# Eight-headed attention: a tile's rows are turned and its logits formed two units on instead of three, in batches of 4, 4, 3, 2, 1, 1, 1 tiles

## The chip, the cores and the metric

The kernel runs on one core of a Trainium2 chip. The metric is the device time of one execution in microseconds, the median of several runs. A core has TensorE (PE, matmuls), VectorE (DVE), ScalarE (ACT), GpSimd (POOL) and SyncE (SP, which here only issues DMAs). Each works through its own queue in order; they meet by semaphores.

## The reference

The whole is a small network on x, 8 x 256 rows of 512 numbers: `x + cross-attention`, `x + gated FFN in fp8`, `x + eight-headed attention`, `x + mixture of experts`. The change lies in the third step and in the routing of the fourth:

```python
def _L1_xattn_ref(q, k, v, gamma):          # eight heads of 32
    qk = jnp.einsum('bhdq,bhdl->bhql', qh, kh) * scale
    sm = jax.nn.softmax(qk, axis=-1)
    ret = jnp.einsum('bhql,bhdl->bhdq', sm, vh)
    return gamma * ret.reshape(B, Dv, Lq)

def _L1_ffn_ref(x, gate_w, gate_b, bias, w1, b1, w2, b2):   # 8 experts, the best 2 of each row
    scores = xf @ gate_w.T + gate_b + bias
    top_scores, top_idx = jax.lax.top_k(scores, TOP_K)
    gates = jax.nn.softmax(top_scores, axis=-1)
    ...
x = x + _L1_xattn_ref(_layernorm(x, axis=-1), ctx_2048, ctx_2048, L1_xattn_gamma)
x = x + _L1_ffn_ref(_layernorm(x, axis=-1), ...)
```

## The kernel before, in words

The kernel has three stages: cross-attention with the FFN (to about 354 us), `head_attention` (to about 655 us) and `experts`. All that follows is in `head_attention`.

x lies in SBUF as `X`, 16 tiles of 128 rows. A **unit** u is the work that updates tile u: four heads at a time (HU = 4) against four chunks of 128 keys (TC = 4), so 16 **steps** (STEPS), worked off in pairs in 8 **cycles** i. A step is one matmul of `scores` into one of two PSUM banks `B[t % 2]`, and an exponential by ScalarE (`weights`) out of it. Every use of B has a number t in the table `turn`, and TensorE may start use t only when ScalarE has finished use t - 2 (semaphore `b_ok`). So `turn` is the order of work on B, and TensorE's and ScalarE's loops must both follow it. Besides the 16 scores, B serves in each unit:

- `mix(u)`, before step 12 (ROWS_AT): the logits of one tile (`logits`, 8 matmuls), the ranks of a batch (`rank`) when one is due, and the turned maxima for the next unit (`rows`);
- `turn_rows(u - 2)`, at the end of unit u: the normalised rows `xn` of tile u - 2 are transposed on TensorE, and ScalarE's `turned_out` copies them to `xt`. The logits of that tile are formed in `mix(u + 1)`, three units after the tile's own.

In the cycles TensorE also does `product` and `row_sums` by turns (the weights times the values, and their sums), and in each odd cycle one `a_quad`: four small matmuls that give the plain scores of a later unit, of which VectorE takes the maxima (`maxima`, two reductions for each quad) before the exponentials need them. In cycles 1 and 3 they are quads 2 and 3 of unit u + 1, in cycles 5 and 7 quads 0 and 1 of unit u + 2. A quad may overwrite its banks only when the maxima of the one before are taken (`max_ok`).

VectorE's order in unit u is: maxima of quad 2; `row_statistics(u - 2)`; maxima of quad 3; `normal_rows(u - 2)`, which writes `xn`; statistics for unit u + 3; maxima of quad 0; `normalise(u - 1)`; maxima of quad 1; queries for unit u + 3; and after that the routing of a batch of tiles, if due: `choose(n)` (the two best experts) in one unit, `gates(n)` and `place_batch(n)` (weights, and the place of each row in its expert's list) in the next. GpSimd adds the result to X (`add`), makes the bf16 parts of queries and keys, gives `1/sqrt` of the variance (`row_power`, between row_statistics and normal_rows), and issues the indirect DMAs that `send` the rows of a batch to `slots_x`, two for each tile. ScalarE's `totals(u - 1)` in cycle 2 empties the bank that `row_sums` of unit u, cycle 3, writes.

The batches before are 4, 4, 3, 3, 1, 1 tiles; the first three are routed inside the loop. The others come behind it, in a tail that ends with `tile_table`, and when the last rows are sent SyncE loads the first tiles of the experts (`load_tile`, a transposing DMA, L1035).

## Time and profile before

| | us |
|---|---|
| median of 3 runs | 848.23 (848.21 to 849.34) |
| profiled execution | 840.42 |
| its span, first to last instruction | 838.7 |
| TensorE busy in the span | 740.9 |
| head_attention, units 2 to 15 | 388.33 to 622.24 |
| its tail, to the first matmul of the experts | 622.24 to 656.95 |

The profile is one execution. A time such as 457.00 is the start of an instruction, counted from the start of the span. An instruction of TensorE that is shown for a group of matmuls has the duration of the group; as matmuls are pipelined, the next group can begin a little before it ends. L1292 and the like are lines of the kernel before.

### The profile page before, as it was taken

How to read it: one execution, taken by the hardware profiler on the slowest of the kernel's cores; microseconds unless marked ns; L12 is line 12 of the kernel's file. 1: busy time of each engine (PE TensorE's matmuls, PEld its weight loads, DVE VectorE, ACT ScalarE, POOL GpSimd, SP SyncE). 2: the span in 40 equal slices, each digit the busy share in tenths (PEclk: the TensorE clock that was granted, in tenths of full speed). 3: DMA queues.
4: the chain of work that ended last, by engine and by line, in shares of the span. 5: the costliest groups of instructions: out<-in, count | busy, mean ns of one | idle time of the engine just before them, and what ended most of it. 6: DMA issues, size and time to landing. Idle time of an engine off the chain costs nothing. (4 is left out here: it accounts for less than half of the span.)

```text
span 838.7 us, 14270 instructions
## 1 busy us (share of the span) xinstructions
PE 740.9 (88%) x4265; PEld 307.1 (37%) x4265; DVE 583.1 (70%) x1096; ACT 399.2 (48%) x744; POOL 358.8 (43%) x356
## 2 busy tenths in 40 slices
PE   3888888799999999798999999989972599999993
PEld 1433433344444444211222222222221355555551
DVE  3577877879594959576888888998947255555552
ACT  1344444365463636256778767866771222222220
POOL 1544455502102031254665668568476033334332
PEclk9899999999999999979999999999995799999998
DMA  7799745002818197134243345444344578999864
GB/s 253 282 131 219 264 174 189 1 0 63 309 59 312 41 344 275 53 92 116 72 112 96 98 128 163 104 116 141 89 160 154 90 106 129 119 134 133 136 88 63
DMA packets 114150, 117.51 MB, mean 140 GB/s; under 512 B 54808, under 2 KB 78232, under 8 KB 113824
## 3 DMA queue, kind: packets, MB, share of 16 engines
q1 hardware_dynamic: 102976, 94.48, 40.4%
q0 software_dynamic: 10384, 22.02, 15.4%
q8 instruction: 36, 0.59, 0.3%
q14 instruction: 34, 0.28, 0.1%
q10 hardware_dynamic: 720, 0.13, 0.1%
HBM read 43.61 MB, written 59.56 MB: 123 GB/s over the span
## 5 line engine op out<-in xcount | busy, mean ns | idle before, releaser
L1397 ACT ACTIVATE t_room<-l_b 128x512 f32<-128x512 f32 x256 | 139.1, 594 | 44.4 <-PE l_b L1292 43.6
L1905 POOL DMA_INDIRECT out<-ex_y,t_tag x39 | 61.7, 1583 | 121.7 <-DMA out<-ex_y,t_tag 70.9
L1801 PE MATMUL ex_hp<-w1h,h_stack 128*128 x312 | 77.2, 317 | 17.2 <-issue 16.7
L1470 DVE TENSOR_REDUCE l_negm<-l_a 128x2 f32<-128x1024 f32 x64 | 75.2, 1219 | 11.1 <-PE l_a L1237 11.1
L1821 PE MATMUL ex_yp<-w2h,ex_ht 128*128 (+1 forms) x234 | 76.2, 380 | 4.9 <-DVE ex_ht L1865 4.7
L1840 ACT ACTIVATE ex_hf<-ex_pre 128x352 f32<-128x352 f32 x39 | 19.4, 496 | 117.1 <-DVE ex_pre L1860 117.1
L1470 DVE TENSOR_REDUCE h_negm<-l_a 128x2 f32<-128x1024 f32 x56 | 65.9, 1220 | 10.5 <-PE l_a L1237 10.3
L1303 PE MATMUL l_pv<-t_room,l_vt 128*32 128x512 f32 x512 | 71.6, 633 | 0.1
L1311 PE MATMUL l_sm<-t_room,ones_f 128*32 128x512 f32 x512 | 69.0, 611 | 0.0
L790 PE MATMUL ps_st<-f_xt,wg 128*128 128x512 fp8e4 x256 | 65.7, 379 | 2.7 <-ACT f_y L838 2.7
L790 PE MATMUL ps_r<-f_xt,wg 128*128 128x512 fp8e4 x256 | 65.7, 379 | 0.0
L936 POOL TENSOR_TENSOR X<-X,f_y 128x512 f32<-128x512 f32 x16 | 19.5, 1221 | 89.9 <-ACT f_y L838 89.9
L1870 DVE TENSOR_TENSOR ex_hl<-ex_hf,ex_hh 128x352 bf16<-128x352 f32 x39 | 20.6, 528 | 43.9 <-ACT ex_hh L1843 42.8
L1801 PE MATMUL ex_hp<-w1l,h_stack 128*128 x156 | 49.4, 317 | 0.0
L823 ACT ACTIVATE f_gate<-ps_st 128x512 bf16<-128x512 f32 x64 | 38.2, 596 | 21.9 <-PE ps_st L790 20.6
L876 DVE TENSOR_TENSOR f_prod<-f_gate,f_up 128x512 bf16<-128x512 bf16 x64 | 26.9, 421 | 29.0 <-ACT f_up L825 26.9
L1292 PE MATMUL l_b<-h_stack 97*128 97x512 bf16 x128 | 42.6, 409 | 3.7 <-DMA h_stack<-h_mrow 2.8
L825 ACT ACTIVATE f_up<-ps_r 128x512 bf16<-128x512 f32 x64 | 38.2, 597 | 15.4 <-PE ps_r L790 15.2
L1821 PE MATMUL ex_yp<-w2l,ex_ht 128*128 (+1 forms) x117 | 44.3, 378 | 0.0
L1878 DVE TENSOR_SCALAR ex_y<-ex_yp,t_tag 128x512 f32<-128x512 f32 x39 | 29.3, 750 | 20.0 <-issue 11.8
L1801 PEld LDWEIGHTS ex_hp<-w1h,h_stack 128*128 128x128 bf16 x312 | 30.9, 99 | 32.0 <-issue 17.5
L1292 PE MATMUL l_b<-l_stack 97*128 97x512 bf16 x128 | 40.3, 385 | 0.8 <-ACT l_xt L1386 0.5
(257 smaller groups left out, 1500.2 us busy)
## 6 DMA issues: line engine op xcount, KB each, us to landing
slots_x<-empty SPq DMA_DIRECT2D x8, 2376.0 KB, 11.0
slots_x<-empty SPq DMA_DIRECT2D x7, 2112.0 KB, 13.0
h_stack<-h_parts SPq DMA_DIRECT2D x96, 64.0 KB
l_stack<-l_parts SPq DMA_DIRECT2D x96, 64.0 KB, 2.0
f_stage<-in_w SPq DMA_DIRECT2D x8, 704.0 KB, 7.2
w1l<-in_ctx SPq DMA_DIRECT2D x8, 512.0 KB, 7.4
f_stage<-in_w SPq DMA_DIRECT2D x8, 512.0 KB
h_kf<-in_ctx SPq DMA_DIRECT2D x16, 256.0 KB, 3.2
```

Source lines behind the costliest of these rows:

```text
L790: mm = pe.matmul(bank[m % 2][:, :], wg8[:, c, col:col + P], xt8[:, c, :], start=c == 0, stop=c == FC - 1)
L823: act.activation(gate[m % 2][:, :], GP[m % 2][:, :], ACT.Gelu_apprx_tanh).then_inc(gate_ok, 1)
L825: act.activation(up[m % 2][:, :], UP[m % 2][:, :], ACT.Copy).then_inc(up_ok, 1)
L1292: pe.matmul(B[t % 2][:, :], stack[u % 2][0:M0 + 1, 0, h, c * P:(c + 1) * P], stack[u % 2][0:M0 + 1, 1, h, :], start=True, stop=True).then_ ...
L1303: mm = pe.matmul(PV[cols, :], VT[u % 2][:, c, cols], weights_at(u, c, h)[:, :], start=c == 0, stop=c == TC - 1)
L1311: mm = pe.matmul(SM[cols, :], ones_f[:, 0:DH], weights_at(u, c, h)[:, :], start=c == 0, stop=c == TC - 1)
L1397: act.activation(weights_at(u, c, h)[:, :], B[t % 2][:, :], ACT.Exp, scale=SCALE).then_inc(b_ok, 1)
L1470: dve.tensor_reduce(negm[u % 2][:, 2 * half:2 * half + 2, j], A[half][:, :, :], AX.X, ALU.max, negate=True)\
L1801: mm = pe.matmul(HP[i % 2][:, 0:H], xt[i % AHEAD][:, xp * FC + f, :], w1p[wp][:, bass.ds(e, 1), f * H:(f + 1) * H], start=k == 0, stop=k = ...
L1821: mm = pe.matmul(YP[i % 2][:, :], ht[i % 2][0:K, n, m, :], w2p[wp][0:K, bass.ds(e, 1), m * D:(m + 1) * D], start=k == 0, stop=k == 3 * HC - 1)
L1878: dve.tensor_scalar(y[i % YS][:, :], YP[i % 2][:, :], tags[i % TAGS][:, bass.ds(e + 1, 1)], None, ALU.mult)\
L1905: pool.indirect_dma_start(out=out, out_offset=bass.IndirectOffsetOnAxis(ap=tags[i % TAGS][:, 0:1].bitcast(U32), axis=0), in_=y[i % YS][:, ...
```

## The change

- The 16 tiles are routed in batches of 4, 4, 3, 2, 1, 1, 1; four of them (INSIDE) within the loop.
- TensorE turns the rows of tile u - 2 before step 6 of unit u (TURN_AT), no longer behind step 15, and ScalarE copies them out there. Their logits are formed in `mix(u)`, not `mix(u + 1)`; `choose`, `gates`, `place_batch`, `gate_weights` and `send` of a batch each come one unit earlier.
- On VectorE `row_statistics(u - 2)` goes ahead of the maxima of quad 2, and `normal_rows(u - 2)` behind them, ahead of the maxima of quad 3.
- On GpSimd `row_power(u - 2)` goes ahead of the sends.
- Behind the loop there is one mix less, and the batches of two, one, one and one are interleaved with the last rows in a new order.

```diff
-    BATCHES = [range(0, 4), range(4, 8), range(8, 11), range(11, 14), range(14, 15), range(15, 16)]
+    BATCHES = [range(0, 4), range(4, 8), range(8, 11), range(11, 13), range(13, 14), range(14, 15), range(15, 16)]
+    INSIDE = 4
+    TURN_AT = 6
 
     turn = {}
     for u in range(NU):
         for s in range(STEPS):
+            if s == TURN_AT and u >= 2:
+                turn["turned", u - 2] = len(turn)
             if s == ROWS_AT:
                 turn["mix", u] = len(turn)
             turn["scores", u, s] = len(turn)
-        if u >= 2:
-            turn["turned", u - 2] = len(turn)
...
     for j in range(NU):
-        turn["logits", j] = turn["mix", j + 3]
-    for n in range(3):
-        turn["ranks", n] = turn["mix", BATCHES[n][-1] + 4]
+        turn["logits", j] = turn["mix", j + 2]
+    for n in range(INSIDE):
+        turn["ranks", n] = turn["mix", BATCHES[n][-1] + 3]
...
@@ tensor @@
+                    if i == TURN_AT // 2 - 1 and u >= 2:
+                        turn_rows(u - 2)
                     if i == ROWS_AT // 2 - 1:
                         mix(u)
-                    if i == CYCLES - 1 and u >= 2:
-                        turn_rows(u - 2)
...
             product(NU - 1, TC - 1)
             row_sums(NU - 1, TC - 1)
+            turn_rows(NU - 2)
+            last_rank(4)
             mix(NU)
-            turn_rows(NU - 2)
-            last_rank(3)
+            turn_rows(NU - 1)
+            last_rank(5)
             mix(NU + 1)
-            turn_rows(NU - 1)
-            last_rank(4)
-            mix(NU + 2)
-            last_rank(5)
+            last_rank(6)
@@ scalar @@
                     weights(u, 2 * i + 1)
+                    if i == TURN_AT // 2 - 1 and u >= 2:
+                        turned_out(u - 2)
...
-                        if i == 7:
-                            turned_out(u - 2)
@@ vector @@
             for u in range(NU):
+                if u >= 2:
+                    row_statistics(u - 2)
                 if u + 1 < NU:
                     maxima(u + 1, 2)
+                if u >= 2:
+                    normal_rows(u - 2)
...
-                if u >= 2:
-                    row_statistics(u - 2)
                 if u + 1 < NU:
                     maxima(u + 1, 3)
-                if u >= 2:
-                    normal_rows(u - 2)
...
-                for n in range(3):
-                    if u == BATCHES[n][-1] + 3:
+                for n in range(INSIDE + 1):
+                    if u == BATCHES[n][-1] + 2:
                         choose(n)
-                    if u == BATCHES[n][-1] + 4:
+                    if n < INSIDE and u == BATCHES[n][-1] + 3:
                         gates(n)
                         place_batch(n)
             row_statistics(NU - 2)
             normal_rows(NU - 2)
-            choose(3)
+            gates(4)
+            place_batch(4)
             normalise(NU - 1)
-            gates(3)
-            place_batch(3)
+            choose(5)
             row_statistics(NU - 1)
             normal_rows(NU - 1)
-            choose(4)
-            gates(4)
-            place_batch(4)
-            choose(5)
             gates(5)
             place_batch(5)
+            choose(6)
+            gates(6)
+            place_batch(6)
             tile_table()
@@ gpsimd @@
                     queries(u + 2)
-                if u == 8:
+                if u >= 2:
+                    row_power(u - 2)
+                if u == 7:
                     pool.wait_ge(cleared, CLEARS)
                 for n in range(3):
-                    first = BATCHES[n][-1] + 5
+                    first = BATCHES[n][-1] + 4
...
-                if u >= 2:
-                    row_power(u - 2)
...
             add(NU - 2)
             row_power(NU - 2)
+            send(3, BATCHES[3])
             with_reciprocals(NU - 1)
-            low_rows(NU - 2)
             add(NU - 1)
             row_power(NU - 1)
-            send(3, BATCHES[3])
+            send(4, BATCHES[4])
+            low_rows(NU - 2)
+            send(5, BATCHES[5])
             low_rows(NU - 1)
-            send(4, BATCHES[4])
-            send(5, BATCHES[5])
+            send(6, BATCHES[6])
```

## Rows read from the trace of the kernel before

**Rows 1.** The page, part 1: busy us (share of the span) and instructions.
```profile
PE 740.9 (88%) x4265; PEld 307.1 (37%) x4265; DVE 583.1 (70%) x1096; ACT 399.2 (48%) x744; POOL 358.8 (43%) x356
```

**Rows 2.** Windows, units 6 to 8: us, busy PE, PEld, DVE, ACT, POOL, PEclk, DMA.
```profile
453.72:469.41 15.69, 15.65 (x115) 4.26 (x111) 12.83 (x17) 12.05 (x25) 9.58 (x12) 1.00 0.42 103
469.41:486.47 17.06, 16.24 (x116) 4.38 (x113) 15.88 (x36) 12.42 (x28) 10.27 (x14) 1.00 0.35 91
486.47:506.11 19.64, 17.63 (x115) 4.41 (x111) 17.39 (x36) 12.12 (x25) 13.49 (x15) 0.91 0.49 138
```

**Rows 3.** Waits of TensorE, 403 to 606 us: total us, times, longest.
```profile
PE l_a L1237 <- DVE l_negm L1470: 3.9, 4, 1.2
```

**Rows 4.** Timeline of TensorE, unit 6, cycles 1 to 3: start, us, instructions.
```profile
457.00 0.39 PE L1237 MATMUL l_a<-l_parts 32*128 32x512 bf16 x4
...
458.86 0.60 PE L1292 MATMUL l_b<-h_stack 97*128 97x512 bf16 x2
459.40 1.06 PE L1311 MATMUL l_sm<-t_room,ones_f 128*32 128x512 f32 x8
```

**Rows 5.** Timeline of VectorE, unit 6, from the maxima of quad 1.
```profile
453.83 2.36 DVE L1470 TENSOR_REDUCE l_negm<-l_a 128x2 f32<-128x1024 f32 x2 [0.96 <-PE l_a L1237]
456.10 0.54 DVE L992 TENSOR_SCALAR h_qf<-X,h_mv,h_rstd 128x512 f32<-128x512 f32 x1
457.43 2.36 DVE L1470 TENSOR_REDUCE l_negm<-l_a 128x2 f32<-128x1024 f32 x2 [0.80 <-PE l_a L1237]
459.70 0.68 DVE L1482 BATCH_NORM_STATS2 l_rst<-X 128x6 f32<-128x512 f32 x1
...
460.83 2.36 DVE L1470 TENSOR_REDUCE l_negm<-l_a 128x2 f32<-128x1024 f32 x2
463.10 0.54 DVE L1493 TENSOR_SCALAR l_xn<-X,l_rmv,l_rrstd 128x512 f32<-128x512 f32 x1
463.55 0.69 DVE L983 BATCH_NORM_STATS2 h_st<-X 128x6 f32<-128x512 f32 x1
```

**Rows 6.** Timeline of GpSimd, unit 6: row_power.
```profile
460.97 0.55 POOL L1663 TENSOR_TENSOR l_rrstd<-l_rveps,neg_half 128x1 f32<-128x1 f32 x1 [2.42 <-DVE l_rveps L1486]
```

**Rows 7.** Timeline of TensorE and ScalarE: totals in unit 6, the turn at its end.
```profile
458.73 0.60 ACT L1408 ACTIVATE l_sums<-l_sm 128x512 f32<-128x512 f32 x1
...
468.49 0.66 PE L1283 MATMUL l_b<-ident_f,l_xn 128*128 128x128 f32 x4
...
469.19 0.60 ACT L1386 ACTIVATE l_xt<-l_b 128x512 f32<-128x512 f32 x1 [0.71 <-PE l_b L1283]
...
469.41 0.82 PE L1292 MATMUL l_b<-l_stack 97*128 97x512 bf16 x2
```

**Rows 8.** Timeline of VectorE: choose(0), gates(0) with place_batch(0), and what follows each.
```profile
472.24 0.80 DVE L1512 TENSOR_TENSOR l_score<-l_score,l_gb 128x32 f32<-128x32 f32 x2
...
474.91 2.35 DVE L1470 TENSOR_REDUCE h_negm<-l_a 128x2 f32<-128x1024 f32 x2
...
489.30 0.18 DVE L1533 TENSOR_TENSOR l_weight<-l_weight,l_both 128x32 f32<-128x32 f32 x1
...
493.17 2.35 DVE L1470 TENSOR_REDUCE l_negm<-l_a 128x2 f32<-128x1024 f32 x2
```

**Rows 9.** Timelines of GpSimd, VectorE and SyncE, the tail: reciprocals, last slots, sends, first load.
```profile
624.36 1.27 POOL L1652 TENSOR_TENSOR l_sr<-l_sums,l_r 128x512 f32<-128x512 f32 x1 [1.02 <-issue]
...
643.48 0.17 DVE L1554 CAST slot<-l_slot_f 128x2 uint32<-128x2 f32 x1
...
646.89 0.97 POOL L1678 DMA_INDIRECT slots_x<-l_kept,slot  x1 [0.30 <-issue]
651.26 2.75 SPq L1035 DMA_TRANSPOSE h_stack<-slots_x  x2
```

**Rows 10.** Windows in unit 8, behind the batch, columns as in rows 2.
```profile
493.20:496.20 3.00, 1.03 (x8) 0.30 (x6) 2.92 (x4) 0.44 (x1) 1.72 (x2) 0.99 0.60 171
496.20:499.40 3.20, 3.20 (x12) 0.33 (x10) 2.60 (x4) 1.84 (x4) 2.56 (x4) 0.50 0.61 224
```

More of the change, by code:

```diff
@@ L1079, in head_attention @@
             turn["scores", u, s] = len(turn)
-        if u >= 2:
-            turn["turned", u - 2] = len(turn)
+    turn["turned", NU - 2] = len(turn)
+    turn["ranks", 4] = len(turn)
     turn["mix", NU] = len(turn)
-    turn["turned", NU - 2] = len(turn)
-    turn["ranks", 3] = len(turn)
+    turn["turned", NU - 1] = len(turn)
+    turn["ranks", 5] = len(turn)
     turn["mix", NU + 1] = len(turn)
-    turn["turned", NU - 1] = len(turn)
-    turn["ranks", 4] = len(turn)
-    turn["mix", NU + 2] = len(turn)
-    turn["ranks", 5] = len(turn)
+    turn["ranks", 6] = len(turn)
     for u in range(1, NU):
@@ L1263, in mix @@
                 wait(pe, b_ok, t - 1)
-                if 0 <= u - 3 < NU:
-                    mm = logits(u - 3, t)
-                for n in range(3):
+                if 0 <= u - 2 < NU:
+                    mm = logits(u - 2, t)
+                for n in range(INSIDE):
                     if turn["ranks", n] == t:
@@ L1361, in mix_out @@
                 act.wait_ge(b_ps, t + 1)
-                if 0 <= u - 3 < NU:
-                    ins = act.activation(score[:, u - 3, :], B[t % 2][:, LOGITS:LOGITS + E], ACT.Copy)
-                for n in range(3):
+                if 0 <= u - 2 < NU:
+                    ins = act.activation(score[:, u - 2, :], B[t % 2][:, LOGITS:LOGITS + E], ACT.Copy)
+                for n in range(INSIDE):
                     if turn["ranks", n] == t:
@@ L1432, in _ @@
                             totals(u - 1)
-                            for n in range(3):
-                                if u == BATCHES[n][-1] + 4:
+                            for n in range(INSIDE):
+                                if u == BATCHES[n][-1] + 3:
                                     gate_weights(n)
@@ L1448, in _ @@
             first_reciprocals(NU - 1)
-            mix_out(NU)
             turned_out(NU - 2)
-            high_rows(NU - 2)
-            gate_weights(3)
-            last_ranks_out(3)
-            mix_out(NU + 1)
-            turned_out(NU - 1)
             gate_weights(4)
             last_ranks_out(4)
-            high_rows(NU - 1)
-            mix_out(NU + 2)
+            high_rows(NU - 2)
+            mix_out(NU)
+            turned_out(NU - 1)
             gate_weights(5)
             last_ranks_out(5)
+            high_rows(NU - 1)
+            mix_out(NU + 1)
+            gate_weights(6)
+            last_ranks_out(6)
         @block.vector
@@ L1609, in _ @@
                     F.queries(dve, X, u + 3)
-                for n in range(3):
-                    if u == BATCHES[n][-1] + 3:
+                for n in range(INSIDE + 1):
+                    if u == BATCHES[n][-1] + 2:
                         choose(n)
-                    if u == BATCHES[n][-1] + 4:
+                    if n < INSIDE and u == BATCHES[n][-1] + 3:
                         gates(n)
```

## The prediction

> **What bounds the kernel now.** I read the page's busy shares first [rows 1]: TensorE is the busiest engine, but an average over four stages says nothing about the stage that is changed. So I cut the attention stage into its sixteen units by the first score matmul of each, and read one window per unit [rows 2]. The reader should see three kinds of unit. Unit 6 lasts 15.69 us and TensorE is busy for 15.65 of them at a granted clock of 1.00; units 3, 4, 5, 9 and 10 read the same. There every microsecond in which TensorE stands still is a microsecond of the kernel. Unit 7 lasts 17.06 and unit 8 19.64 (units 11 and 12 repeat the pair with 17.05 and 19.64; 13 and 14 lie within 0.2 of 15.69). The view of who waited for whom, from unit 3 to the end of unit 14, says why [rows 3]: the quads of a_quad waited for VectorE's maxima, up to 1.2 us at a time, because a batch of the routing arithmetic stands in front of them in VectorE's queue [rows 8]. Those excesses are 2 x (1.37 + 3.95) = 10.6 us in all, and they are what the change could win inside the loop.
>
> **Part 1, the turn at step 6: the transposes now meet a row that isn't ready.** This part decides. Both chains hang on the same fixed points of TensorE, so I laid them over unit 6.
>
> VectorE [rows 5]: the maxima of quad 1 start at 453.83, the queries at 456.10, and these leave the engine free 0.46 later (the step from 463.10 to the next instruction is 0.45 for the same kind), at 456.56. The change puts row_statistics here; it takes 460.83 - 459.70 = 1.13, so to 457.69. Then come the maxima of quad 2, 459.70 - 457.43 = 2.27, to 459.96, and only then normal_rows, 0.54, to 460.50. GpSimd's row_power comes between: it takes 0.55 [rows 6] and has the 2.27 of the maxima to hide under, with the queries' parts ahead of it in its queue already under way since 456.6.
>
> TensorE [rows 4]: it starts quad 2 at 457.00 and the score matmuls of steps 6 and 7 at 458.86. There the change puts turn_rows, which waits for xn. The turn no longer stands at the end of the unit before, whose effect on the scores was a gap of 0.82 - 0.60 = 0.22 (the normal pair takes 0.60) [rows 4, 7], so TensorE comes to the turn at 458.64. It waits until 460.50 plus 0.05 for the signal: 1.91 us. Even if VectorE took the row statistics for nothing, the maxima could start at 457.43 and the wait would be 1.6. Nothing can hide it, since turn_rows is in order with everything behind it: scores of steps 6 to 15, product, row_sums, mix and the next quads, and through them ScalarE's exponentials.
>
> Behind the turn its evacuation is late too. Today ScalarE starts xt 0.70 after the turn began [rows 7]; an activation frees ScalarE about 0.56 later; and an a_quad covers 0.33 of it. In the new place no a_quad follows (they come only on odd i) and totals(u-1) is queued behind turned_out on ScalarE, while row_sums waits for totals. From the turn's start: xt 0.70 to 1.30, totals to 1.86, row_sums at 1.90, where work alone would bring TensorE there at 1.13. Today totals ends at 459.33 and row_sums starts at 459.40 [rows 4, 7], so there is no slack to take this up. Cost 0.77, less the 0.22 that goes: 0.55.
>
> Together 1.91 + 0.55 = 2.46 us in each of units 2 to 14, thirteen: 32.0. In unit 15 nothing is left of the maxima, and by the same laying over the row is there in time; only 0.55 stays. Sum 32.5 us.
>
> **Part 2, the batches.** choose of four tiles holds VectorE from 472.24 to 474.91, 2.67 us; gates with place_batch from 489.30 to 493.17, 3.87 us [rows 8]. Both stand after the queries and so before row_statistics and maxima of quad 2: in the new order they lie wholly on the path to xn. Batches of four fall into units 6 and 7, 10 and 11; the batch of three into 13 and 14, estimated at three quarters, 2.0 and 2.9. Sum 2 x (2.67 + 3.87) + 4.9 = 18.0. The old excesses of 10.6 go, since while TensorE stands at the turn VectorE catches up and the quads find their banks free. The rest of the split (two tiles, then one, one, one) is in the tail. Net +7.4.
>
> **Part 3, the sends on GpSimd.** They move behind row_power and one unit forward; each takes 0.97 with 0.30 in front of it [rows 9], so four take 5.1 and the six of batch 2 take 7.6. What stands behind them now is keys(u+3), with_reciprocals and F.power. Keys have a unit of slack, and with_reciprocals would end before VectorE comes to normalise, the unit being 2.5 us longer. I cost this at nothing; with the cover gone it is at most what is over in three units, some 1 us.
>
> **Part 4, the tail.** Today the last transposed load starts at 651.26, 3.40 after the last send ended (646.89 + 0.97), and the sends queue on GpSimd behind one another; the last slots are there at 643.65 [rows 9]. From these slots to the end of the sends it is 4.2 us now, as four sends and low_rows queue there; the change leaves two sends behind them, 2.5 us, which by itself wins 1.7. But it puts four sends (5.1 us) ahead of with_reciprocals(15), which began at 624.36; started behind row_power(14) at about 624.5 they push it to 629.6, and the chain to the last row (normalise, add, statistics) loses the delays by choose(3) and gates(3) that it has today, some 3 us. Net between -1.5 and +1.5: I take 0.
>
> **Part 5, the clock.** In unit 8 TensorE worked 1.03 of 3.00 us and the next 3.20 us ran at a granted clock of 0.50, that is the 1.2 GHz level instead of 2.4 [rows 10]; for a fully busy engine this costs half of it, 1.6 us. In unit 7, whose excess is 1.37, it stayed at 1.00 [rows 2]. The new wait of 1.91 with 0.77 in pieces behind it lies between. I let it fall in all six units with a batch in front of the row (waits of 3.9 to 5.8) and in half of the six others that don't fall today: 6 x 1.6 + 3 x 1.6 = 14.4 us. The Trainium skill, "TensorE: Matmul & The Clock Gate", section "A second HAM failure mode: psum-queue depth-cycling", says that frequent short idles between groups of matmuls are enough to make the clock swing between its levels; that speaks against this change, and by it the usual units fall too, each at the row's 1.6. No row of before has a wait of this size alone, so the trace neither confirms nor denies it.
>
> **Sum.** 32.5 + 7.4 + 0 + 0 + 14.4 = 54.3 us. The profiled execution had a span of 838.7 and a time of 840.4; the median of the runs is 848.2, so I carry the difference over: 840.4 + 54.3 = 894.7 for a profiled one, 848.2 + 54 = 902 for the median.
>
> **The rivals.**
> 1. The clock stays up in the usual units, or everywhere: 54.3 - 4.8 = 49.5, or 54.3 - 14.4 = 39.9, less up to 3 if normal_rows is always at its shortest: 885 to 898. For it: unit 7.
> 2. The clock falls in every unit, and GpSimd's accesses stretch normalise so that quad 1's maxima start 0.5 late: 54.3 + 4.8 + 6 = 65: 908 to 913. For it: rows 10, where about 2 us of idle time was enough.
> 3. Faster. The row is on time: it would need xn before 458.64, that is row_statistics and normal_rows both done before the maxima of quad 2, which VectorE's order as written doesn't do. From that point on the wait is nothing, the batches cost no more than today's 10.6 less what the catch-up saves; with all of it won and the late evacuation paid in 14 units: 14 x 0.55 - 10.6 = -2.9, 845. Against it: both chains hang on TensorE's own quads, so no slack elsewhere moves them apart.
> 4. The wait is there only behind a batch (VectorE gains on TensorE otherwise): 7.4 + 7.7 + 9.6 = 25, 873; or the turn is hidden behind something I don't see and nothing moves: 848.
>
> **How the numbers follow.** Forecast 0.58, rival 1 0.18, rival 2 0.15, rival 3 0.03, rival 4 0.05 with 873 and 0.01 with no change. The likeliest is 902. The range takes in rivals 1 and 2, with some microseconds for the tail and for batch work that may be covered below: 879 to 916. What a measurement of this kernel can tell from no change is about 0.2%, 1.7 us. Faster 0.03, same 0.01, slower 0.96.
>
> **What would show it.** In the profile after, turn_rows waits for VectorE's xn in units 2 to 14, about 1.9 us in a usual one and 4 to 6 in those of a batch; the quads no longer wait for the maxima; a usual unit lasts 18 to 20 us; row_sums waits for totals; the granted clock has a stretch of 0.50 in at least six units; the experts' stage is unchanged in length. The prediction is wrong if xn is ready when TensorE reaches the turn, if a usual unit is below 17 us, or if the units with a batch are no longer than the others.

## The result, and the profile of the kernel after

| | before | after |
|---|---|---|
| median of 4 runs, us | 848.64 (848.21 to 849.34) | 909.83 (907.45 to 911.12) |
| ratio, 95% interval | 1 | 1.0714 (1.068 to 1.0749) |
| profiled execution, span | 838.7 | 905.7 |
| units 2 to 14 | 217.3 | 278.0 |
| unit 15, to the end of the last row_sums | 16.6 | 16.9 |
| tail, from there to the first transposed load | 29.0 | 35.8 |
| from that load to the end | 187.4 | 189.4 |

The changed kernel is 61 us slower, inside the range and 8 us above the forecast of 902. The spans differ by 67.0 us: +60.8 in units 2 to 14, +0.3 in unit 15, +6.8 in the tail, +2.0 in the experts, and -2.9 ahead of unit 2. They differ by more than the medians because the profiled execution of the kernel before, 840.4 us, is 8 us below its median here. (The kernel before has a median of 848.6 on this chip and 839.6 to 849.1 on the four others used below; the changed one, run again on one of these, kept its time, so that there it costs 70 us.) The last two differences need not be the change's: in a second profile of the changed kernel (run 1) unit 2 starts at 388.07, where it starts at 388.33 before and at 385.47 here; and the experts' stage, which the runs below don't touch, takes 187.7 to 191.3 us in them.

The busy times hardly move, as a comparison with [rows 1] shows. Part 1 of the page of the kernel after:

```profile
PE 752.0 (83%) x4238; PEld 308.5 (34%) x4267; DVE 581.7 (64%) x1110; ACT 398.1 (44%) x747; POOL 357.0 (39%) x356
```

TensorE is busy 11 us more, and VectorE, ScalarE and GpSimd are not. The 11 are a balance: in units 2 to 14 TensorE is busy for 226.3 us where it was for 209.1, and ahead of unit 2 for 5 less. Of these 17 us the logits of tile 0, which now fall into unit 2, make 1; the other operations are the same ones at a lower clock. The rest of what these units grew by, 43.6 of 60.8 us, is idle time. Windows of the kernel after, units 4 to 7, columns as in [rows 2]:

```profile
427.72:445.95 18.23, 15.67 (x114) 4.23 (x111) 13.27 (x18) 11.97 (x24) 9.60 (x11) 1.00 0.33 85
445.95:465.64 19.69, 17.16 (x114) 4.29 (x110) 13.31 (x18) 12.04 (x24) 9.60 (x11) 0.91 0.30 83
465.64:489.12 23.48, 18.51 (x116) 4.75 (x113) 15.88 (x37) 12.37 (x27) 9.63 (x11) 0.85 0.27 68
489.12:513.22 24.10, 18.03 (x115) 4.68 (x111) 16.80 (x37) 12.04 (x24) 13.83 (x15) 0.86 0.36 113
```

Three kinds again, but not those of before. In unit 4 TensorE works 15.67 us as it did in 15.65, at full clock, and the unit is 2.54 longer: that is the bare price of the new wait. Unit 5 has the same wait and a clock of 0.91. Units 6 and 7 carry the batch: 23.48 and 24.10 for 15.69 and 17.06, at 0.85 and 0.86. The view of the waits of TensorE from 400 to 680 says what the waiting is:

```profile
PE l_b L1284 <- DVE l_xn L1492: 33.5, 9, 5.8
PE l_b L1284 <- issue: 7.8, 3, 4.0
PE l_b L1293 <- ACT l_xt L1386: 4.9, 13, 0.5
```

L1284 is turn_rows: twelve waits for the normalised row, 41.3 us (three of them the view can't put down to an instruction; xn ends 0.05 or 0.06 us ahead of each of these turns too). L1293 is the score matmul behind it, which waits for ScalarE's xt 13 times, 0.26 us in the units with a batch and 0.47 in the others. From unit 3 on no quad waits for maxima any more: the group of [rows 3] is gone. In unit 2, ahead of this view, two still do, 1.41 and 0.74 us (1.26 and 0.74 before). The timelines of unit 5 show one wait whole; TensorE, VectorE, GpSimd and ScalarE in turn (start, us, instruction, idle time before it):

```profile
449.34 0.60 PE L1293 MATMUL l_b<-l_stack 97*128 97x512 bf16 x2
449.88 1.07 PE L1304 MATMUL l_pv<-t_room,l_vt 128*32 128x512 f32 x8
452.97 0.65 PE L1284 MATMUL l_b<-ident_f,l_xn 128*128 128x128 f32 x4 [2.02 <-DVE l_xn L1492]
453.46 0.38 PE L1293 MATMUL l_b<-l_stack 97*128 97x512 bf16 x1
454.31 0.45 PE L1293 MATMUL l_b<-l_stack 97*128 97x512 bf16 x1 [0.47 <-ACT l_xt L1386]
...
449.01 0.68 DVE L1481 BATCH_NORM_STATS2 l_rst<-X 128x6 f32<-128x512 f32 x1
...
450.11 2.35 DVE L1469 TENSOR_REDUCE h_negm<-l_a 128x2 f32<-128x1024 f32 x2
452.37 0.54 DVE L1492 TENSOR_SCALAR l_xn<-X,l_rmv,l_rrstd 128x512 f32<-128x512 f32 x1
...
450.97 0.56 POOL L1661 TENSOR_TENSOR l_rrstd<-l_rveps,neg_half 128x1 f32<-128x1 f32 x1
...
453.66 0.60 ACT L1386 ACTIVATE l_xt<-l_b 128x512 f32<-128x512 f32 x1 [2.80 <-PE l_b L1284]
```

The row's variance power is ready at 451.53, in the middle of the maxima; what the row waits for is the end of the maxima. The wait was worked out from [rows 4, 5] at 1.91 and is 2.02. What it starts from had moved a little: the maxima of quad 1 begin 0.34 us into unit 5 (0.11 in [rows 5]), because normalise ahead of them takes 1.37 us, and 0.68 ahead of unit 6 before. It does so in units 2 to 13 of the kernel after, here beside GpSimd's low_rows (VectorE and GpSimd):

```profile
445.00 1.37 DVE L1475 SCALAR_TENSOR_TENSOR l_pvs<-l_sr,l_pvs 128x512 f32<-128x512 f32 x1
...
444.66 1.16 POOL L1665 TENSOR_TENSOR l_kept<-l_xn,l_kept 128x512 bf16<-128x512 f32 x1 [1.64 <-ACT l_kept L1391]
```

Two windows of unit 5, behind that wait, columns as in [rows 2]:

```profile
452.90:455.50 2.60, 2.02 (x10) 0.78 (x14) 0.01 (x1) 1.84 (x4) 0.00 (x0) 0.81 0.42 101
455.50:459.00 3.50, 3.50 (x22) 0.40 (x14) 1.69 (x2) 1.88 (x5) 1.48 (x2) 0.65 0.25 75
```

The granted clock goes to its lower level (1.2 GHz for 2.4) for some 3 us, as in the second window of [rows 10], after a wait of 2.0 and a piece of 0.47; [rows 10] had about 2 us of idle time in its first window.

### The profile page after: what moved, and what is told of

It reads as the page before. It is cut to its first block and busy times, and to the rows that moved or that the text cites. A ratio compares the mean times of both kernels' runs of the same rounds, so it can differ in the third digit from the quotient of the medians.

```text
span 905.7 us, 14264 instructions
## 1 busy us (share of the span) xinstructions
PE 752.0 (83%) x4238; PEld 308.5 (34%) x4267; DVE 581.7 (64%) x1110; ACT 398.1 (44%) x747; POOL 357.0 (39%) x356
## 5 line engine op out<-in xcount | busy, mean ns | idle before, releaser
L1312 PE MATMUL l_sm<-t_room,ones_f 128*32 128x512 f32 x512 | 76.8, 675 | 0.6
L1820 PE MATMUL ex_yp<-w2h,ex_ht 128*128 (+1 forms) x215 | 68.9, 380 | 4.0 <-DVE ex_ht L1864 3.9
L1284 PE MATMUL l_b<-ident_f,l_xn 128*128 128x128 f32 x64 | 13.7, 351 | 60.7 <-DVE l_xn L1492 53.0
L1293 PE MATMUL l_b<-h_stack 97*128 97x512 bf16 x128 | 45.4, 428 | 6.8 <-DMA h_stack<-h_mrow 2.8
L1869 DVE TENSOR_TENSOR ex_hl<-ex_hf,ex_hh 128x352 bf16<-128x352 f32 x39 | 20.5, 526 | 43.9 <-ACT ex_hh L1842 43.9
L1293 PE MATMUL l_b<-l_stack 97*128 97x512 bf16 x128 | 43.6, 414 | 2.9 <-ACT l_xt L1386 2.7
L1877 DVE TENSOR_SCALAR ex_y<-ex_yp,t_tag 128x512 f32<-128x512 f32 x39 | 29.3, 751 | 20.8 <-issue 13.3
```

Source lines behind the costliest of these rows:

```text
L1293: pe.matmul(B[t % 2][:, :], stack[u % 2][0:M0 + 1, 0, h, c * P:(c + 1) * P], stack[u % 2][0:M0 + 1, 1, h, :], start=True, stop=True).then_ ...
L1312: mm = pe.matmul(SM[cols, :], ones_f[:, 0:DH], weights_at(u, c, h)[:, :], start=c == 0, stop=c == TC - 1)
L1820: mm = pe.matmul(YP[i % 2][:, :], ht[i % 2][0:K, n, m, :], w2p[wp][0:K, bass.ds(e, 1), m * D:(m + 1) * D], start=k == 0, stop=k == 3 * HC - 1)
L1877: dve.tensor_scalar(y[i % YS][:, :], YP[i % 2][:, :], tags[i % TAGS][:, bass.ds(e + 1, 1)], None, ALU.mult)\
```

## The experiments

My theory: the whole loss inside the loop comes from xn, which VectorE gives 2 us too late for a turn at step 6 (and 4 to 6 us too late behind a block of routing), and each such wait costs again through the clock. Rivals: the place of the turn costs by itself; the routing costs wherever it stands; the tail is something else. Each kernel has its time beside the kernel before on the same chip; where I compare with the changed kernel, its 909.7 us are from run 1 and so, for runs 2, 3, 4, 8, 9 and the first kernel of 6, from another chip. The length of units below is from one profiled execution each, from first score matmul to first score matmul.

**1. The changed kernel again**, beside the kernel before on another chip (the chip of runs 5 and 7 and of the second kernel of 6).

> The changed kernel itself, beside the others on the same chip: 1.07 times the kernel before, as in the result.

909.68 us, ratio 1.0835 (1.0801 to 1.0869). The units repeat: usual ones 17.9 to 20.2, those with a batch 23.4 to 24.5 apart from unit 14 (21.5), and 52.8 us from the start of unit 15 to the first load, as in the first profile. Which of the usual units lose their clock differs (here 3, 5, 9 and 12, in the first profile 3, 5, 8 and 12). This is the reference for what follows.

**2. The logits of rows that aren't normalised**: the turn stays before step 6 but reads X, which is complete long before; the routing is computed on the wrong rows, nothing else is left out.

```diff
-                pe.wait_ge(xn_ok, j + 1)
+                pe.wait_ge(res_ok, j + 1)
...
-                    mm = pe.transpose(B[t % 2][:, f * P:(f + 1) * P], xn[:, f * P:(f + 1) * P], ident_f[:, :])
+                    mm = pe.transpose(B[t % 2][:, f * P:(f + 1) * P], X[:, j, f * P:(f + 1) * P], ident_f[:, :])
```

> The changed kernel, but the turn takes the rows of X as they are, and waits for add(u-2) only, not for the row statistics and xn. So the logits are those of rows that are not normalised, and the routing and the output are others; read the units of the attention stage alone. It separates the wait for xn from what the place of the turn costs by itself. Theory: the wait is gone, the evacuation stays late by 0.55 us, a usual unit lasts 16.2 to 16.3 us at a clock of 1.00. Rival 1 (no cost of the place by itself): 15.7. Rival 2 (the place costs most of it): above 17.5. Units with a batch as in the run with the turn in cycle 4, 17.5 to 21.5.

855.86 us (one run, beside 840.7 for the kernel before), 54 us below the changed kernel. Usual units last 16.17 to 16.23 at a clock of 1.00: so the place of the turn costs 0.5 us a unit and the wait for xn, at full clock, the other 2.0. Units 2 to 14 are still 12.9 us longer than before, so my theory's "whole loss" is too much: half of that is the 0.5, the rest lies in the units with a batch (19.66 and 20.30 for units 6 and 7), where quads wait for the maxima again. What is left behind the turn is this line of TensorE's timeline in unit 5:

```profile
445.05 0.39 PE L1293 MATMUL l_b<-l_stack 97*128 97x512 bf16 x1 [0.47 <-ACT l_xt L1386]
```

**3. The wait filled.** TensorE gets extra matmuls into a bank that the turn overwrites, 8 in a usual unit and 16 to 24 in one with a batch, ahead of its wait for xn. They are about as long as the wait and change no result.

```diff
                 t = turn["turned", j]
+                pe.wait_ge(b_ok, t - 1)
+                if j + 2 < NU - 1:
+                    u = j + 2
+                    for _ in range({6: 18, 7: 24, 10: 18, 11: 24, 13: 16, 14: 16}.get(u, 8)):
+                        pe.matmul(B[t % 2][:, :], stack[u % 2][0:M0 + 1, 0, 0, 0:P], stack[u % 2][0:M0 + 1, 1, 0, :], start=True, stop=True)
                 pe.wait_ge(xn_ok, j + 1)
-                pe.wait_ge(b_ok, t - 1)
```

> The changed kernel with extra matmuls (128 x 512 bf16, into the bank that the transposes then overwrite) between the scores and the wait for xn: 8 in a usual unit, 18, 24, 18, 24, 16, 16 in units 6, 7, 10, 11, 13, 14. They use the waiting time and change no result. Theory (the clock is 1.5 us of each usual unit where it falls and about 2.2 us of each unit with a batch): the granted clock stays at 1.00 in units 3 to 14, a usual unit lasts 18.2 to 18.3 us like unit 4 of the changed kernel, and the whole 890 to 896 us. Rival (the low clock lies in the idle time and costs little; the units that last longer do so by longer waits): 907 us or more, or longer still by the extra matmuls.

889.16 us, ratio 1.0589 (1.0554 to 1.0624): 20.5 us below the changed kernel for work that computes nothing, and 1 below what I had expected. The granted clock is 1.00 in every unit from 3 to 14. Every usual unit is now 18.27 to 18.42, the price of unit 4 above without the clock's; units 6 and 7 are 21.5 and 21.7 for 23.5 and 24.1. The clock's part of the loss is about 20 us, where Part 5 had 14.4: 20.5 by the medians, 18.7 by the profiles of units 3 to 14 (19.0 against run 1's).

**4. The turn before step 10** (TURN_AT = 10 for 6), four steps more for xn to come.

> The changed kernel with TURN_AT 10 for 6: the rows are turned in cycle 4, 3.4 us of TensorE's work later, and still before the mix that forms their logits. Theory (TensorE waits for xn): xn is ready 6.75 us into a usual unit and TensorE is there at about 8.6, so the wait of 2.0 us and the falls of the clock in the usual units go; a usual unit lasts 15.8 to 16.2 us. In the units with a batch the quads wait for the maxima again, as before the change and somewhat longer, as the row statistics stand ahead as well: 17.5 to 18.5 and 20 to 21.5. With the tail as in the changed kernel 860 to 870 us. Rival (turning rows in mid-unit costs by itself, through the evacuation by ScalarE and the order of the B banks): a usual unit stays above 17.5 us and the kernel above 885.

880.97 us, ratio 1.0497 (1.0445 to 1.0548); the whole is 11 to 21 us above what I had expected. The usual units are right, 16.00 to 16.26. The units with a batch are not: 24.46 and 21.75 for units 6 and 7. With the wait at the turn gone, VectorE has no time to catch up, and the quads wait again. Timeline of TensorE, unit 6, and the windows behind it:

```profile
461.51 0.39 PE L1238 MATMUL l_a<-l_parts 32*128 32x512 bf16 x2 [1.58 <-DVE l_negm L1469]
462.64 0.61 PE L1238 MATMUL l_a<-l_parts 32*128 32x512 bf16 x2 [0.74 <-DVE l_negm L1469]
```

```profile
459.80:462.60 2.80, 0.52 (x6) 0.10 (x2) 2.63 (x6) 1.17 (x3) 0.56 (x1) 0.94 0.42 90
462.60:466.00 3.40, 3.36 (x12) 0.43 (x12) 3.30 (x4) 1.09 (x2) 1.77 (x2) 0.50 0.38 100
466.00:469.40 3.40, 3.14 (x18) 1.16 (x14) 0.34 (x2) 2.09 (x4) 0.99 (x1) 0.50 0.00 0
469.40:472.80 3.40, 3.40 (x24) 2.08 (x16) 0.00 (x0) 0.06 (x1) 2.01 (x3) 0.50 0.00 0
472.80:475.60 2.80, 2.80 (x14) 0.40 (x10) 2.25 (x2) 2.02 (x7) 0.10 (x1) 0.50 0.27 27
475.60:478.00 2.40, 2.40 (x19) 0.48 (x16) 1.64 (x3) 1.08 (x2) 1.85 (x3) 0.93 0.50 189
```

2.3 us of waits, and then 13 us at the lower level although TensorE is busy in nearly all of them: some 6 us lost for 2.3 (the unit is 8.4 longer than a usual one). That is far above the 1.6 that [rows 10] gave as the price of one fall, and it is what I had wrong here. The stops themselves don't tell when it comes. Unit 2 of the same execution, 385.85 to 405.06, has nearly the same two, and its granted clock is 1.00 throughout (TensorE):

```profile
390.58 0.39 PE L1238 MATMUL l_a<-l_parts 32*128 32x512 bf16 x2 [1.60 <-DVE l_negm L1469]
391.71 0.39 PE L1238 MATMUL l_a<-l_parts 32*128 32x512 bf16 x2 [0.74 <-DVE l_negm L1469]
```

**5. The batches in the middle.** The changed kernel with choose, and a unit later gates and place_batch, of the first three batches behind the maxima of quad 3: a block of routing then stands behind normal_rows, no longer ahead of it. gate_weights and the sends follow.

```diff
                 if u + 1 < NU:
                     maxima(u + 1, 3)
+                for n in range(3):
+                    if u == BATCHES[n][-1] + 3:
+                        choose(n)
+                    if u == BATCHES[n][-1] + 4:
+                        gates(n)
+                        place_batch(n)
...
-                for n in range(INSIDE + 1):
+                for n in range(3, INSIDE + 1):
                     if u == BATCHES[n][-1] + 2:
                         choose(n)
```

> The changed kernel with the routing of batches 0, 1 and 2 moved on VectorE from the end of a unit to the place behind the maxima of quad 3, where VectorE stands idle in the changed kernel while TensorE waits for the row (choose one unit later by name, the weights' exponential and the sends with it). Theory (a batch between the queries and the row statistics lies wholly on the path to xn): the waits of 4.7 and 5.8 us in units 6, 7, 10, 11, 13, 14 become 2.0 like the others, these units last 18.2 to 19.9 us instead of 21.5 to 24.6, and the whole is 20 to 24 us shorter than the changed kernel on the same chip. Rival (VectorE's total work is what counts, so its place changes nothing): within 3 us.

900.54 us, ratio 1.0722 (1.0659 to 1.0785): 9 us below the changed kernel, less than half of what I had expected. The waits at the turn fell as the theory has it, to 2.02 and 1.79 in units 6 and 7, and units 7 and 11 to 20.8. But units 6 and 10 stayed at 23.8 and 24.0. Timeline of TensorE, unit 6:

```profile
476.74 0.66 PE L1284 MATMUL l_b<-ident_f,l_xn 128*128 128x128 f32 x4 [2.02 <-DVE l_xn L1494]
...
486.50 0.21 PE L1258 MATMUL l_b<-l_both,l_before 128*128 128x32 bf16 x1 [2.48 <-DVE l_both L1525]
```

L1258 is rank, in the mix, which needs the result of the choose that I had moved. A new wait in place of the old one. In units 7 and 11 quad 1 waits for maxima, 1.31 and 0.74 us, and units 8 and 12 behind them have a clock of 0.86 and 0.85. And the way from unit 15 to the first load has become 2.5 us longer (55.3 for 52.8).

**6. The tail in the order of before** (first low_back, one line; then tail_back, the sends too).

```diff
+            with_reciprocals(NU - 1)
+            low_rows(NU - 2)
+            add(NU - 1)
+            row_power(NU - 1)
             send(3, BATCHES[3])
-            with_reciprocals(NU - 1)
-            add(NU - 1)
-            row_power(NU - 1)
             send(4, BATCHES[4])
-            low_rows(NU - 2)
-            send(5, BATCHES[5])
             low_rows(NU - 1)
+            send(5, BATCHES[5])
```

> The changed kernel with one step of GpSimd's tail put back: low_rows(14) ahead of add(15), no longer behind row_power(15) and the sends of tile 13. Theory: VectorE's normal_rows(15) waits for lo_ok, that is for low_rows(14), and the change moved this behind two sends; in the changed kernel's trace GpSimd's row_power(15) ends at 696.79 and xn starts only at 700.69, 3.9 us later. Undone, the tail is 3.5 us shorter (3.9 less the 0.3 to 0.4 by which add(15) comes later): 906.3 us where the changed kernel has 909.8. Rival: the sends ahead of with_reciprocals(15) are what lengthens the tail, and GpSimd does the same work either way: within 0.5 us of 909.8.

> The changed kernel with GpSimd's tail in the old manner: the reciprocals of unit 15, low_rows(14), add(15), row_power(15), and only then the sends of batch 3 and after. It undoes both suspected steps, of which the run low_back undid one (there 2.4 us of the tail in the trace). Theory: the four sends ahead of with_reciprocals(15) are the larger rest of the 6.8 us by which the tail grew; from the last row_sums to the first load of the experts it takes 29 to 31 us instead of 35.8, and the whole is 5 to 7 us shorter than the changed kernel on the same chip. Rival (the sends only move and the last load waits for the last of them either way): 2 to 3 us shorter, as low_back.

907.38 and 905.40 us (1.0812, 1.0773 to 1.0852, and 1.0774, 1.0733 to 1.0816): the totals alone can't tell these apart from the changed kernel, 1.0835 (1.0801 to 1.0869). The traces can. From the start of unit 15 to the first load it is 45.7 us before, 52.8 in the changed kernel, 50.2 with low_rows back, and 48.8 with the sends back too. So 4.0 of the 7.1 us come from these two, 2.6 from low_rows and 1.4 from the sends, less than I expected of either. Most of the 3 us that remain can be read from the traces, though no run takes them away. VectorE in the kernel after:

```profile
681.99 0.69 DVE L1481 BATCH_NORM_STATS2 l_rst<-X 128x6 f32<-128x512 f32 x1
```

That is row_statistics(14), 1.55 us behind the last row_sums (680.44). Its tile was complete at 679.74; VectorE was still in gates(3), place_batch(3) and choose(4), which the new batches put ahead of it and which hold it from 676.42 to 681.99. In tail_back it is the same, 1.53 behind. Before, row_statistics(14) started at 621.52, 0.7 us ahead of the last row_sums, as soon as its tile was complete. That is 2.3 us of the 3.

**7. The kernel before, with the routing cut up**: choose in two parts (the second behind normal_rows a unit later), gates at the end of a unit, place_batch in the next; on GpSimd row_power goes ahead of the sends. A try for a version that beats the kernel before.

```diff
+            def choose(n):
+                choose_1(n)
+                choose_2(n)
...
                 if u >= 2:
                     normal_rows(u - 2)
+                for n in range(3):
+                    if u == BATCHES[n][-1] + 4:
+                        choose_2(n)
+                    if u == BATCHES[n][-1] + 5:
+                        place_batch(n)
```

> The kernel before (rows turned at the end of a unit, three units on), with the routing of batches 0 to 2 cut up on VectorE: the first half of choose at the end of a unit, the second behind normal_rows of the next, the gates at the end of that one, place_batch behind normal_rows of the one after; row_power ahead of the sends. Theory: the kernel before loses 10.6 us in units 7, 8, 11, 12 only because 2.7 and 3.9 us of routing stand in one piece in front of the maxima of quad 2; in pieces of at most 2.1 us most of this goes and the clock doesn't fall: 6 to 9 us shorter than the kernel before, 0.990 to 0.993 of it. Rival (VectorE's work in these units is too much wherever it stands): same as before, 0.998 to 1.002.

861.31 us, ratio 1.0254 (1.0215 to 1.0293), wrong in sign. Units 7 and 8 are 20.69 and 20.88 for 17.06 and 19.64. In units 7, 11 and 14 it is the wait of run 5 once more, since rank needs the second part of choose. In units 8 and 12 it is another: ScalarE's high_rows (L1391) stands until a kept tile has been sent, and TensorE's turn behind it. TensorE in units 7 and 8, then ScalarE:

```profile
482.69 0.19 PE L1257 MATMUL l_b<-l_both,l_before 128*128 128x32 bf16 x1 [2.79 <-DVE l_both L1531]
...
508.31 1.08 PE L1283 MATMUL l_b<-ident_f,l_xn 128*128 128x128 f32 x4 [3.82 <-ACT t_room L1397]
...
507.05 0.63 ACT L1391 ACTIVATE l_kept<-l_xn 128x512 bf16<-128x512 f32 x1 [4.18 <-DMA slots_x<-l_kept,slot]
```

Run 8 meets the same edge and says more of it.

**8. The batches in the middle and the ranks later**: run 5 with the ranks of the two batches of four formed one mix later, placed one unit later, and the sends behind with_reciprocals; and **9.** the same with the turn before step 10 and the tail of tail_back.

```diff
-        turn["ranks", n] = turn["mix", BATCHES[n][-1] + 3]
+        turn["ranks", n] = turn["mix", BATCHES[n][-1] + (4 if n < 2 else 3)]
...
+                    if u == BATCHES[n][-1] + (5 if n < 2 else 4):
+                        place_batch(n)
```

> The changed kernel with the routing of the first three batches in the middle of VectorE's unit (behind the maxima of quad 3, a unit later), as in the run batch_mid, but the ranks of the batches of four are formed one mix later still and placed one unit later, and the sends stand behind with_reciprocals. Theory: what batch_mid left in the units of the first half of a batch (23.8 us) is only TensorE's wait of 2.5 us for choose inside the mix and the slow clock behind it; with the ranks later that wait is gone, so units 6, 7, 10 and 11 all last 18.2 to 20.8 us, and the whole is about 18 us below the changed kernel: a ratio to the kernel before of 1.058 to 1.068. Rival: VectorE's 2.7 us of choose in the middle make some engine wait wherever they stand (the quads, or normalise); then units 6 and 10 stay above 22 us and the ratio is 1.070 to 1.080, as in batch_mid.

> The same, with the turn before step 10 and not 6 (usual units then 16.1 us, as in the run turn10), and the last rows' work in the order of the run tail_back. Theory, from both parts added up: usual units 16.1, units of a batch 16.5 to 19, tail about 49 us from the start of unit 15 to the experts; together a ratio to the kernel before of 1.005 to 1.025. Rival: with no slack given by the wait at the turn, choose in the middle makes the quads wait for the maxima and the clock falls behind it, as it did in turn10; then units 6 and 10 are above 21 us and the ratio is 1.030 to 1.050.

Run 8: 906.45 us, ratio 1.0697 (1.065 to 1.0743), 3 us below the changed kernel where I had expected 18, between the theory's 1.068 and the rival's 1.070 and a miss for both mechanisms as told. Units 6 and 7 did what I wanted, 20.30 and 18.82; the wait in the mix is gone. But unit 8 went to 24.80. Timelines of TensorE and ScalarE around its end:

```profile
529.53 1.01 PE L1293 MATMUL l_b<-l_stack 97*128 97x512 bf16 x2 [3.54 <-ACT t_room L1397]
...
528.27 0.63 ACT L1391 ACTIVATE l_kept<-l_xn 128x512 bf16<-128x512 f32 x1 [4.62 <-DMA slots_x<-l_kept,slot]
```

L1391 is high_rows. The rows of six tiles are kept (KEPT = 6), and tile 6 overwrites tile 0, whose place is now computed, and whose rows are sent, a unit later: ScalarE stands 4.62 us with the exponentials queued behind, and TensorE 3.54. A longer ring wasn't tried. Units 10 and 11 have 23.68 and 21.33, unit 10 with quads that wait 1.14 and 0.74 for maxima, as the rival said.

Run 9: 864.57 us, 1.0195 (1.0149 to 1.024), as the theory had it, and the best version that forms the logits two units on: usual units 16.0 to 16.7, units 6 and 7 at 18.51 and 16.16 with a clock of 1.00. Units 8 and 12, at 20.0 and 19.7, have the ring's wait, and unit 13 lasts 21.0 at a clock of 0.79. It is still 15.5 us above the kernel before on its chip: 0.4 in every usual unit, these three units, and 53.2 us from the start of unit 15 to the first load, where I had expected 49 and the kernel before has 45.7.

**10. The kernel before, gates one gap earlier.** The block of 3.87 us in [rows 8] becomes two: gates behind normalise, place_batch where it was.

```diff
                 if u:
                     normalise(u - 1)
+                for n in range(3):
+                    if u == BATCHES[n][-1] + 4:
+                        gates(n)
...
                     if u == BATCHES[n][-1] + 4:
-                        gates(n)
                         place_batch(n)
```

> The kernel before with one edit: gates of a batch stand one gap earlier in VectorE's unit, behind normalise and ahead of the maxima of quad 1, and place_batch stays behind the queries; nothing that TensorE itself waits for (choose, the ranks) moves. Theory: VectorE has about 0.9 to 1.0 us free ahead of the maxima of quads 1 and 2, what a block of routing takes beyond that stops TensorE, and only the stop of about 2 us behind gates with place_batch (3.87 us in one block) drops the clock. In two blocks of 2.1 and 1.8 us the stops are about 1.2 and 0.8 us, the clock stays up, units 8 and 12 last 17.5 to 18.0 us and not 19.64, and the whole is 3 to 4.5 us shorter: ratio to the kernel before 0.994 to 0.997. Rival: the late normalise or GpSimd's DMA descriptors stretch what is moved, or two stops drop the clock as one does; then units 8 and 12 stay at 19 us or more and the ratio is 1.000 to 1.006.

840.43 us, ratio 1.0005 (0.9989 to 1.0021), no difference: the rival's figure. Units 8 and 12 last 20.22 and 20.17 for 19.64. Timeline of TensorE in unit 8, and the windows behind it:

```profile
492.06 0.39 PE L1237 MATMUL l_a<-l_parts 32*128 32x512 bf16 x2 [1.21 <-DVE l_negm L1470]
493.20 0.39 PE L1237 MATMUL l_a<-l_parts 32*128 32x512 bf16 x2 [0.74 <-DVE l_negm L1470]
```

```profile
490.50:493.20 2.70, 0.75 (x7) 0.10 (x4) 2.67 (x5) 0.79 (x2) 1.13 (x1) 1.00 0.55 139
493.20:496.40 3.20, 3.20 (x14) 0.49 (x14) 2.86 (x5) 1.60 (x3) 2.56 (x3) 0.65 0.58 216
496.40:499.50 3.10, 3.10 (x24) 1.30 (x22) 2.03 (x5) 1.08 (x2) 2.99 (x5) 0.81 0.37 134
```

Two stops of 1.21 and 0.74 behind one another, which the smaller second block still makes, drop the clock as the one block did; unit 8 of the kernel before has the same pair, 1.23 and 0.74. They are the same because the maxima of quad 2 start no earlier: 7.22 us into unit 8, and 6.70 before. Gates ahead of quad 1's maxima hold these and the queries up, and the second block wasn't small. Timelines of VectorE and GpSimd:

```profile
487.99 0.51 DVE L1548 TENSOR_TENSOR l_place<-l_ranks,l_carry 128x8 f32<-128x8 f32 x1
488.42 0.15 DVE L1549 TENSOR_TENSOR l_carry<-l_carry,l_counts 128x8 f32<-128x8 f32 x1
488.61 1.13 DVE L1548 TENSOR_TENSOR l_place<-l_ranks,l_carry 128x8 f32<-128x8 f32 x1
...
487.87 0.61 POOL L1647 CAST h_parts<-h_qf 128x512 bf16<-128x512 f32 x1 [3.20 <-DVE h_qf L992]
488.56 1.16 POOL L1013 TENSOR_TENSOR h_parts<-h_qf,h_parts 128x512 bf16<-128x512 f32 x1
```

Of eight equal additions two take 0.51 and 1.13 us where the others take 0.15 to 0.17, and each of the two ends when an operation of GpSimd ends, 488.48 and 489.72. place_batch took 3.1 us and not the 1.76 that it takes in the trace of before (491.41 to 493.17, the end of the block in [rows 8]). The Trainium skill, "SBUF — State Buffer", section "SBUF: two separate sides", says that a VectorE operation with two inputs in SBUF and a GpSimd operation that reads SBUF exclude each other for a whole instruction; the two additions agree with it, 0.51 and 1.13 against operations of 0.61 and 1.16. No version that I ran beats the kernel before.

## Why the prediction was right, and where it was off

**The wait, Part 1: right.** Predicted 1.91 + 0.55 = 2.46 us in a unit; units 4 and 9, where the clock stayed up, are 2.54 and 2.59 longer. The two parts are 2.0 and 0.5 in them; that quad 1's maxima begin some 0.25 late was not in the sum. Run 2 takes away the wait alone and finds the same split, 0.5 for the place and 2.0 for the wait. One detail shows elsewhere than I had put it: not row_sums behind totals but the next score matmul behind xt is what stops, for 0.47. In unit 15 no wait was predicted and none is there; the unit is 0.3 longer, not 0.55.

**The batches, Part 2: right.** The waits at the turn are 4.71 and 5.81 in units 6 and 7, 4.69 and 5.83 in 10 and 11, against 1.91 + 2.67 and 1.91 + 3.87, that is 4.58 and 5.78. Units 13 and 14 had 4.44 and 3.99, for 3.9 and 4.8; the estimate by three quarters was wrong in each and right in the sum. From unit 3 on no quad waits for maxima. Run 5 shows the cause by removing it: with the block behind the row the waits are 2.02 and 1.79.

**The sends in the loop, Part 3: right**, as far as it shows. In run 3, where the clock stays up, units 2 to 14 are 41.8 us longer than before; Parts 1 and 2 make 39.4 of them and unit 2 another 1.4 (below), so about 1 us is left for all else.

**The clock, Part 5: the mechanism right, the term mis-sized.** Units 2 to 14 grew by 60.8 us; less 32.0 and 7.4 that leaves 21.4. But 1.6 of it, in unit 2, is not the clock's. Its granted clock is 0.91 before and 0.92 after, with one fall in each, so no new one came. TensorE forms the logits of tile 0 there, a unit earlier than before, and that is work of about 1.1 us that my sum by waits didn't hold:

```profile
402.83 1.06 PE L1251 MATMUL l_b<-l_gw,l_xt 128*128 128x8 f32 x8
```

The rest are waits a few tenths longer than in the other units. So the clock took 19.8 us where I had 14.4, and run 3 gives 18.7 to 20.5 by another way. Of the six usual units four fell, not three, at 1.2 to 1.8 us each, 6.4 for 4.8 with the small rest of the two others. The six with a batch cost 13.3 for 9.6: my 1.6 was for one fall each, as [rows 10] shows it, and a wait of 4 to 6 us with a longer stretch behind it costs more (by their granted clocks of 0.85 and 0.91 the lower level lasts some 7 us in unit 6 and 3.5 in unit 5). In unit 7 of the kernel after, the windows behind the wait of 5.81 read:

```profile
496.20:501.00 4.80, 1.07 (x5) 0.85 (x5) 3.51 (x6) 0.00 (x0) 2.78 (x3) 0.78 0.50 152
501.00:506.00 5.00, 4.74 (x21) 0.71 (x23) 1.22 (x2) 3.25 (x7) 2.92 (x4) 0.53 0.44 162
```

The five microseconds at 0.53, with 4.74 of work, alone cost some 2.2. The rule of the Trainium skill that I had weighed against the sum ("TensorE: Matmul & The Clock Gate", section "A second HAM failure mode: psum-queue depth-cycling", that frequent short idles make the clock swing) went the right way: taken to the letter, all six usual units fall, and four did. By the granted clock of run 2, pieces of 0.47 alone do not bring it down.

**The tail, Part 4: two waits missed.** I had it between -1.5 and +1.5 and it is +6.8. The 3 us that I let it win by losing choose(3) and gates(3) came back at another place, as gates(3), place_batch(3) and choose(4) ahead of row_statistics(14), 2.3 us (run 6). The four sends ahead of with_reciprocals were in the sum, the late start wasn't: row_power(14) comes at 683.26, 2.8 us behind the last row_sums, and the sends end at 689.13. And one edge was missing altogether: low_rows(14) stands behind two sends now, and normal_rows(15) may overwrite xn only behind low_rows(14). GpSimd's and VectorE's timelines of the kernel after:

```profile
696.22 0.57 POOL L1661 TENSOR_TENSOR l_rrstd<-l_rveps,neg_half 128x1 f32<-128x1 f32 x1 [2.45 <-DVE l_rveps L1485]
697.03 1.04 POOL L1676 DMA_INDIRECT slots_x<-l_kept,slot  x1 [0.24 <-issue]
698.38 0.98 POOL L1676 DMA_INDIRECT slots_x<-l_kept,slot  x1 [0.31 <-issue]
699.39 1.16 POOL L1665 TENSOR_TENSOR l_kept<-l_xn,l_kept 128x512 bf16<-128x512 f32 x1
...
700.69 0.55 DVE L1492 TENSOR_SCALAR l_xn<-X,l_rmv,l_rrstd 128x512 f32<-128x512 f32 x1 [4.54 <-POOL l_kept L1665]
```

Everything for the row is there at 696.79, and it waits 3.9 us for a subtraction of the tile before. With low_rows back in its old place the row comes at once; the two kernels of 6 put the two terms at 2.6 and 1.4 us.

**The sum.** 54.3 was forecast for the profiled execution; 67.0 is what the spans show: 5.4 more of clock, 1.6 in unit 2, 6.8 of tail, 2.0 in the experts' stage (which I said wouldn't change; other profiles scatter by as much), less 2.9 ahead of unit 2, where the change does nothing, and 0.2 less than forecast in unit 15. The range held it because it took in the clock's fall everywhere; that the median came out only 8 above the forecast owes something to the kernel before being slow on that chip, for on the chip of run 1 the change costs 70. Rival 1 falls by run 1 and the clocks of both profiles, rival 3 and rival 4 by the waits at L1284 in every unit from 2 to 14. Rival 2's total, 908 to 913, is the one that the median meets, and half of its mechanism is there: normalise is stretched and quad 1's maxima are late, but by some 0.25 us and not 0.5, and this lies inside the waits of 2.0. Not all units fell; its total was made up by longer falls and by the tail.

## What to carry to other kernels

Before a step is moved ahead in an engine that sets the end, write down when its operand is ready as counted from that same engine's work: here a 2.3 us reduction stood between the two, and no slack of the other engines could hide it. Then follow every buffer that the moved steps write or free, with its ring and its next writer; four of the new waits here (rank behind choose, high_rows behind the send, normal_rows behind low_rows, the quads behind the maxima) were such edges, and each ate what the move was to win. And price a stop of TensorE with its clock: here 13 waits of 1.6 to 5.8 us came to 43.6 us by themselves and to 19 or 20 more through what ran slowly behind them.

## What the runs showed of the hardware that I had not expected

- The clock's fall hasn't one price. After 2.02 us of waiting it was about 3 us at the lower level (1.5 us lost, unit 5 after); after 1.58 + 0.74 us it was 13 us, with TensorE busy in 12.7 of the 13.0 (run 4, windows 462.6 to 475.6); and after 1.60 + 0.74 us in unit 2 of run 4 it was nothing. No run separates what decided.
- Waits of 1.6 to 2.2 us dropped the clock in four of six equal units and not in the other two, and two runs of the same kernel differ in which; the shortest single one that did was 1.61 (unit 12 after, clock 0.91). Of pairs of stops, 0.62 and 0.74 us were enough in unit 6 of run 2 (0.91) and 1.21 and 0.74 in unit 8 of run 10, while 1.44 and 0.74 in unit 2 of run 10 were not, nor what stopped unit 7 before, with an excess of 1.37 in all. So no length of stop tells the fall from these traces.
- Matmuls that compute nothing made the kernel 20 us faster (run 3), by keeping the clock up.
- A VectorE addition of 128 x 8 numbers takes 0.15 us, but 1.13 where it starts with an operation of GpSimd and ends with it (run 10). The tail of the kernel after has two such, 1.14 and 1.21. In run 10 this took place_batch from 1.8 to 3.1 us. Larger operations do the same: normalise, 128 x 512, takes 0.69 us, and 1.37 where low_rows is already under way (445.00 in the kernel after).
